# Last steps of a two-layer mixture kernel in another order: the first layer of tiles 30 and 31 half a step ahead, the last convolution and the last h1 product moved forward

## What is computed

```
x  = x + y0 + sum_e alpha_e * (z_e @ B0_e)       # u = x @ [A0 | W0], then mixed over channels per batch
c1 = conv(x) + beta1                             # windows of 12 neighbours, 4 output phases
h1 = c1 @ [A1 | gate]                            # 224 low-rank columns and 28 logits
x  = x + c1 @ W1 + (gate * h1) @ B1
```

## Time and profile before

| what | value |
|---|---|
| median of 3 runs | 404.41 us (402.56 to 407.03) |
| profiled execution, its own time | 404.12 us |
| its span, first to last instruction | 402.3 us |
| mean granted TensorE clock | 0.981 of full |
| PE busy | 382.8 us (95%) |
| DVE busy | 288.2 us (72%) |
| ACT busy | 125.1 us (31%) |

### The profile page before, as it was taken

The page is one execution under the profiler, slowest core; times in us unless marked ns, Lnnn a source line. Parts: engine busy times, 40 slices in busy tenths (PEclk is TensorE's granted clock), DMA queues, the critical chain, the costliest instruction groups (busy, mean ns, idle before and its releaser), DMA issues.

```text
span 402.3 us, 9559 instructions
## 1 busy us (share of the span) xinstructions
PE 382.8 (95%) x3187; PEld 335.7 (83%) x3187; DVE 288.2 (72%) x979; ACT 125.1 (31%) x384; POOL 19.8 (5%) x95
## 2 busy tenths in 40 slices
PE   5977799999999999999999999999999999999976
PEld 4877787888889888888888898888888889877755
DVE  5547688777778777777777887777777778677854
ACT  5335533332233332233222333222332233222310
POOL 5200000000000000000000000000000000000000
PEclk9998879999999999999999999999999999999999
DMA  7756426476777776666677677666666776766651
GB/s 229 230 163 154 94 70 132 122 175 156 181 171 169 183 178 134 164 160 164 150 175 183 156 183 181 155 149 160 160 159 165 179 170 144 159 157 150 142 106 52
DMA packets 70716, 62.97 MB, mean 157 GB/s; under 512 B 3823, under 2 KB 53199, under 8 KB 70570
## 3 DMA queue, kind: packets, MB, share of 16 engines
q1 hardware_dynamic: 70696, 62.74, 64.1%
q10 hardware_dynamic: 2, 0.00, 0.0%
HBM read 45.69 MB, written 16.91 MB: 156 GB/s over the span
## 4 chain that ended last, share of the span: by engine, by line
PE 84%; DVE 7%; DMA 5%; ACT 2%; issue 1%; SPq 1%; DVEq 0%; ACTq 0%
PE p_chy L853 13%; PE p_chy L847 13%; PE p_chy L848 13%; PE p_u L847 9%; PE p_u L853 8%; PE p_u L848 8%; PE p_chy L983 8%; PE p_t L996 3%; DMA win<-x_scratch 3%; PE p_y L847 2%; PE p_y L848 2%; PE p_y L853 2%; DVE mix L623 1%; DMA w_sb<-in_w 1%; DMA x_scratch<-x 1%
## 5 line engine op out<-in xcount | busy, mean ns | idle before, releaser
L847 PE MATMUL p_u<-w_hi,xt_hi 128*128 128x256 f32 (+1 forms) x256 | 72.0, 307 | 2.5 <-DVE w_lo L609 2.5
L848 PE MATMUL p_u<-w_lo,xt_hi 128*128 128x256 f32 (+1 forms) x256 | 69.6, 297 | 0.0
L717 DVE STREAM_TRANSPOSE c<-p_chy 128x512 f32<-128x512 f32 x32 | 22.9, 717 | 56.6 <-PE p_chy L983 56.2
L480 ACT CAST u_hi<-p_u 128x256 fp32r<-128x256 f32 x64 | 24.8, 387 | 107.1 <-PE p_u L853 107.1
L847 PEld LDWEIGHTS p_u<-w_hi,xt_hi 128*128 128x128 f32 x256 | 50.6, 198 | 3.5 <-DVE w_lo L609 1.8
L525 ACT CAST g1t_hi<-p_t 113x256 fp32r<-113x256 f32 x32 | 11.9, 373 | 125.4 <-PE p_t L996 125.4
L848 PEld LDWEIGHTS p_u<-w_lo,xt_hi 128*128 128x128 f32 x256 | 50.7, 198 | 0.0
L847 PE MATMUL p_chy<-w_hi,c_hi 128*128 128x512 f32 x124 | 49.3, 397 | 0.0
L848 PE MATMUL p_chy<-w_lo,c_hi 128*128 128x512 f32 x124 | 48.8, 394 | 0.0
L853 PE MATMUL p_u<-w_hi,xt_lo 128*128 128x256 f32 (+1 forms) x256 | 44.3, 297 | 1.4 <-DVE xt_lo L590 1.4
L983 PEld LDWEIGHTS p_chy<-win,wc_sb 96*32 96x32 f32 x1024 | 26.7, 111 | 17.4 <-issue 12.8
(11 more groups left out here) (165 smaller groups left out, 747.5 us busy)
## 6 DMA issues: line engine op xcount, KB each, us to landing
win<-x_scratch SPq DMA_DIRECT2D x96, 256.0 KB, 4.4
x_scratch<-x SPq DMA_DIRECT2D x32, 260.0 KB, 2.1
xt_sb<-in_xt SPq DMA_DIRECT2D x32, 256.0 KB, 5.3
x_sb<-in_x SPq DMA_DIRECT2D x32, 256.0 KB, 5.3
out<-y_sb SPq DMA_DIRECT2D x32, 256.0 KB, 4.5
w_sb<-in_w SPq DMA_DIRECT2D x4, 256.0 KB, 5.3
w_sb<-in_w SPq DMA_DIRECT2D x1, 1024.0 KB, 7.4
a_sb<-in_a SPq DMA_DIRECT2D x1, 504.0 KB, 3.9
```

The source lines that it names most:

```text
L480: nc.scalar.copy(u_hi[:, t.mod(4), cols], p_u[:, banks]).then_inc(u_hi_done[half], 1)
L717: V.transpose(c1[:], p_cv).then_inc(c1_tr, 1)
L847: mm(psum, lhs_hi, rhs_hi, start=start and n == 0, stop=False)
L848: mm(psum, lhs_hi, rhs_lo, start=False, stop=False)
```

## The change

It touches steps 29 to 34 only; the instructions are the same, in another order. In PE's queue:

- `mixing(30)` moves from the head of step 30 to the end of step 29, between `conv(28)` and `transpose_g1(27)`; `mixing(31)` moves from the head of step 31 into step 30, between the hi and the lo passes of `base_1(28)`.
- In steps 30 and 31 `transpose_g0(s)` now comes right behind `low_rank_1(s-3)`, then `lows_1(s-2)`, then `low_rank_0(s)`, and `base_1(s-2)` only behind that.
- In step 32 `conv(31)` comes right behind `low_rank_1(29)`, ahead of `lows_1(30)` and `base_1(30)`; `lows_1(31)` moves from step 33 into step 32, ahead of `transpose_g1(30)`.
- In step 33 `low_rank_1(30)` lies between the hi and lo passes of `base_1(31)`, and `transpose_g1(31)` behind both.

In DVE's queue `residual(30)` and `residual(31)` move ahead of the chain from L795 to L820 of their step; the layer-0 part of tile 31 (L726 to L750) moves from the head of step 31 to the end of step 30; the transpose and remainder of `c1` of tile 31 move from step 33 to step 32, ahead of the chain of tile 30; `g1t_lo` of tile 30 moves into the chain of tile 31. In ACT's queue the exponent of tile 31 (L533) moves to the end of step 30, and `c1_hi` of tile 31 to step 32. SP's and POOL's queues are as before. In the diff, the part left out on DVE only wraps the instructions of L714 to L750 into functions `c1_transposed`, `c1_low`, `g1t_low`, `z0_logits` and `g0_scaled`.

```diff
--- before.py
+++ after.py
@@ -523,15 +523,24 @@
                 if (s + -3).live():
                     after(act, g1_tr, s, -3)
                     nc.scalar.copy(g1t_hi[:], p_g1t).then_inc(g1t_hi_done, 1)
-                if (s + -LAG).live():
-                    v = s + -LAG
+                def c1_high(v):
+
                     after(act, c1_tr, v)
                     after(act, y1_mm, v, -2)
                     nc.scalar.copy(by_group(c1_hi[:, v.mod(2)]), by_phases(c1)).then_inc(c1_hi_done, 1)
-                if s.live():
-                    after(act, z0_nmax_done, s)
+
+                def z0_exponent(v):
+
+                    after(act, z0_nmax_done, v)
                     nc.scalar.activation(z0_exp[:], by_slot(z0[:])[:, :, R], ACT.Exp, bias=z0_nmax[:],
                                          accum_out=z0_sum[:]).then_inc(z0_exp_done, 1)
+
+                if (s + -LAG).live() and not is_last(s + -LAG):
+                    c1_high(s + -LAG)
+                if is_last(s + -1):
+                    c1_high(s + -1)
+                if s.live() and not is_last(s):
+                    z0_exponent(s)
                 early = at(s, 0) or at(s, 1)
                 if not early and (s + 2).live():
                     mix_high(s + 2)
@@ -549,6 +558,8 @@
                     after(act, ntop_done, s, -LAG)
                     nc.scalar.activation(t_exp[:], top[:, 0:2], ACT.Exp, bias=ntop[:],
                                          accum_out=t_sum[:]).then_inc(t_exp_done, 1)
+                if at(s, NT - 2):
+                    z0_exponent(s + 1)
                 if t.live():
                     u_high(t, "a")
                 if at(s, 0):
...
+
+                ahead = at(s, NT - 2) or is_last(s)
+                if (s + -LAG).live() and not is_last(s + -LAG):
+                    c1_transposed(s + -LAG)
+                if (s + -3).live() and not is_last(s + -LAG):
+                    g1t_low(s + -3)
+                if s.live() and not is_last(s):
+                    z0_logits(s)
+                    if at(s, 0):
+                        mix_low(s + 1)
+                if (s + -LAG).live() and not is_last(s + -LAG):
+                    c1_low(s + -LAG)
+                if s.live() and not is_last(s):
+                    g0_scaled(s)
                 if at(s, 0):
 
                     u_low(s + 1, "b")
@@ -776,6 +803,11 @@
                     u_low(s + 3, "a")
                 if (s + -3).live() and not is_last(s + -LAG):
                     output(s + -3)
+                if ahead:
+                    residual(s)
+                if is_last(s + -1):
+                    c1_transposed(s + -1)
+                    c1_low(s + -1)
                 early = at(s, 0) or at(s, 1)
                 if not early and (s + 4).live():
                     xt_low(s + 4)
@@ -803,6 +835,8 @@
                     V.max_index(top_i[:], top[:], h1[:, L1N:H1N]).then_inc(top_i_done, 1)
                     after(dve, top_i_done, v)
                     V.tensor_copy(top_f[:], top_i[:, 0:2]).then_inc(top_f_done, 1)
+                    if is_last(v):
+                        g1t_low(s + -3)
                     after(dve, t_exp_done, v)
                     V.reciprocal(t_rec[:], t_sum[:]).then_inc(t_rec_done, 1)
                     after(dve, t_rec_done, v)
@@ -823,10 +857,13 @@
                                     ALU.mult).then_inc(g1_done, 1)
                 if is_last(s + -LAG):
                     output(s + -3)
+                if at(s, NT - 2):
+                    z0_logits(s + 1)
+                    g0_scaled(s + 1)
                 if not early and (s + UA).live():
                     u_low(s + UA, "b")
                     u_low(s + UA, "a")
-                if not early and s.live():
+                if not early and not ahead and s.live():
                     residual(s)
                 if at(s, 2):
                     dve.wait_ge(b1_hi_done, 1)
@@ -1028,23 +1065,47 @@
                     between()
                     lo_passes(y1_bank(v), full, False)
 
-                if s.live():
+                if at(s, NT - 3):
                     mixing(s)
-                if is_last(s + -LAG):
-
+                    low_rank_1(s + -3)
                     lows_1(s + -LAG)
+                    transpose_g0(s)
+                    base_1(s + -LAG, lambda: low_rank_0(s))
+                    conv(s + -1)
+                    mixing(s + 1)
+                    transpose_g1(s + -LAG)
+                elif at(s, NT - 2) or is_last(s):
                     low_rank_1(s + -3)
-                    base_1(s + -LAG, lambda: transpose_g1(s + -LAG))
+                    transpose_g0(s)
+                    lows_1(s + -LAG)
+                    low_rank_0(s)
+                    if is_last(s):
+                        base_1(s + -LAG)
+                    else:
+                        base_1(s + -LAG, lambda: mixing(s + 1))
+                    conv(s + -1)
+                    transpose_g1(s + -LAG)
+                elif is_last(s + -1):
+                    low_rank_1(s + -3)
+                    conv(s + -1)
+                    lows_1(s + -LAG)
+                    base_1(s + -LAG)
+                    lows_1(s + -1)
+                    transpose_g1(s + -LAG)
+                elif is_last(s + -LAG):
+                    base_1(s + -LAG, lambda: low_rank_1(s + -3))
+                    transpose_g1(s + -LAG)
                     low_rank_1(s + -LAG)
                 else:
-                    if (s + -3).live() and not is_last(s + -3):
+                    if s.live():
+                        mixing(s)
+                    if (s + -3).live():
                         low_rank_1(s + -3)
                     if (s + -LAG).live():
                         lows_1(s + -LAG)
                     early = at(s, 0) or at(s, 1)
                     t = s + (s.c + 1 if early else UA)
-                    running = t.live()
-                    if running:
+                    if t.live():
                         u_half(t, "b")
                         transpose_g0(s)
                         u_half(t, "a")
@@ -1056,20 +1117,13 @@
                                 pe.wait_ge(rsw0_done, 1)
                                 column_sums(p_rs1, P, a1_hi, a1_lo).then_inc(rs1_mm, 1)
                             u_half(t + 1, "a")
-                    elif s.live():
-                        transpose_g0(s)
                     if at(s, 2):
                         pe.wait_ge(w1_lo_done, 1)
                         after(pe, c1_tr, s, -2)
                         column_sums(p_rsw1, 1, w1_hi, w1_lo).then_inc(rsw1_mm, 1)
                     if (s + -LAG).live():
-                        if not running and s.live():
-                            base_1(s + -LAG, lambda: low_rank_0(s))
-                        elif is_last(s + -1):
-                            base_1(s + -LAG, lambda: conv(s + -1))
-                        else:
-                            base_1(s + -LAG)
-                    if (s + -1).live() and not is_last(s + -1):
+                        base_1(s + -LAG)
+                    if (s + -1).live():
                         conv(s + -1)
                     if (s + -LAG).live():
                         transpose_g1(s + -LAG)
```

More of the change, by code:

```diff
@@ L709, in residual, with c1_transposed @@
                                     x_sb[:, v.mod(4), :].rearrange("p (f q) -> p f q", f=NPH), ALU.add).then_inc(x1_done, 1)
-                if (s + -LAG).live():
-                    v = s + -LAG
+                def c1_transposed(v):
                     after(dve, cv_mm, v)
@@ L717, in step, with c1_low @@
                     V.transpose(c1[:], p_cv).then_inc(c1_tr, 1)
-                if (s + -3).live():
-                    after(dve, g1t_hi_done, s, -3)
-                    V.tensor_tensor(g1t_lo[:], p_g1t, g1t_hi[:].bitcast(f32), ALU.subtract).then_inc(g1t_lo_done, 1)
-                if s.live():
[L723 to L733, removed]
+                def c1_low(v):
                     after(dve, c1_hi_done, v)
@@ L736, in step, with g1t_low, z0_logits @@
                                     by_group(c1_hi[:, v.mod(2)].bitcast(f32)), ALU.subtract).then_inc(c1_lo_done, 1)
-                if s.live():
-                    after(dve, z0_exp_done, s)
+                def g1t_low(v):
+                    after(dve, g1t_hi_done, v)
+                    V.tensor_tensor(g1t_lo[:], p_g1t, g1t_hi[:].bitcast(f32), ALU.subtract).then_inc(g1t_lo_done, 1)
+                def z0_logits(v):
+                    after(dve, z0_mm, v)
+                    if at(v, 0):
+                        dve.wait_ge(z_add_done, 1)
+                    V.tensor_tensor(z0[:], p_z0, z_add[:, v.n(), :], ALU.add).then_inc(z0_done, 1)
+                    after(dve, z0_done, v)
+                    V.tensor_reduce(z0_nmax[:], by_slot(z0[:])[:, :, R], X, ALU.max, negate=True).then_inc(z0_nmax_done, 1)
@@ L739, in step, with g0_scaled @@
+                def g0_scaled(v):
```

(11 more changed lines are left out.)

1 line of the change is left out of this document (removed).

## The result

| | before | after |
|---|---|---|
| median of 20 runs each | 404.46 us | 408.27 us |
| ratio after / before | | 1.0095, 95% interval 1.0069 to 1.012 |
| profiled execution / its span | 404.12 / 402.3 us | 412.1 / 410.2 us |
| `conv(28)` to the last y_sb, in the profile | 37.15 us | 42.06 us |

A forecast was written before the change was run, and what follows sets the result against it. PE, busy 95% of the span, was taken as the bound through how its in-order queue is filled. The forecast was 404.12 + 2.2 (order) + 1.6 (clock) = 407.9 us, range 404.3 to 409.9.

The forecast's parts named there:

- End of step 29 and step 30: low_rank_1(27) starts 0.94 us after transpose_g1(27); PE then idles 0.86 us ahead of transpose_g0(30), waiting for DVE's g0s.
- Step 31: g1t_lo(28) queues behind tile 31's z0 work on DVE; low_rank_0(31) starts near 378.05, 0.4 us later than before.
- Tile 31's hand-over: residual(31) ends 0.4 us earlier, at 379.2; 8.35 us of store, issues and landing lead to conv(31) at 387.55.
- the rival of earlier windows: Windows land earlier than 8.35 us after x1, near 386, hiding the extra work; time 404.8 us, chance 0.09.
- Step 32: PE idles 2.6 us ahead of conv(31); from there 13.75 us to y_sb, against 11.16 before.
- The order term: Last y_sb comes 2.2 us later, at 401.3, from the new block order and its waits.
- The clock term: The 2.6 us idle at conv(31) drops the clock to half rate for 3.4 us, costing 1.6 us.
- the long one: Low clock for 6.8 us from the wait at conv(31), costing 3.4 us; time 409.7 us, chance 0.08.
- The sum: The profiled execution's 404.12 us plus 2.2 for order and 1.6 for the clock, giving 407.9 us.
- The clock staying up: The wait at conv(31) is shorter or brings no clock drop; time 406.3 us, chance 0.27.
- The half step is really won: The 3.0 us of new waits vanish and low_rank_0(31) starts at 375.05; time 403.3 us, chance 0.06.
- its break-even: low_rank_0(31) starting at 375.9, with fixed lengths of 23.2 us from there to y_sb.

The follow-up runs named there:

- The run with the covers put back: The half step alone, with transpose_g1(27) before mixing(30), lows_1(28) before transpose_g0(30), low_rank_0(30) amid the hi passes; 404.01 us against 404.22, ratio 1.000.
- the kernels with 0.40 and 1.33 us of idle: The change with ten unused matmuls ahead of conv(31), ratio 1.0053; the change with lows_1(30) ahead of conv(31), ratio 1.0055.
- the filled kernel: The change with ten unused 512-wide matmuls between low_rank_1(29) and conv(31); 405.73 us, ratio to before 1.0053; again 406.22 us, ratio 1.0043.
- the three edits: Kernel before with residual(s) amid the gate chain, low_rank_0(s) amid the hi passes, tile 31's c1_hi and c1_lo earlier; 400.67 us, again 400.52.
- the half step alone: The change with PE steps 32 and 33, and tile 31's c1 work on ScalarE and VectorE, as before; 403.23 us against 403.33, ratio 1.0024.

## Why the prediction held, and where a size was off

- **End of step 29 and step 30: right.** `low_rank_1(27)` started 0.84 after `transpose_g1(27)` (0.94 foreseen) and waited 0.46; the idle ahead of `transpose_g0(30)` was 0.72, foreseen as 0.86, and released by DVE's `g0s`.
- **Step 31: right in mechanism, a little too dark.** `g1t_lo(28)` stood behind tile 31's `z0` work; `low_rank_0(31)` came 0.2 later than before, not 0.4. The run with the covers put back shows that these waits, and no transfer, held it.
- **Tile 31's hand-over: right.** From the end of the residual, 381.92, to `conv(31)` at 390.34 it took 8.42; I had 8.35. `conv(31)` came 0.55 earlier than before against 0.4 foreseen. The output store was issued at 380.35 and x1's at 381.94, and its price was indeed near nothing. This also answers the rival of earlier windows: they landed no sooner after x1 than before.
- **Step 32: right.** Idle 2.71 against 2.6. From `conv(31)` to the last y_sb at full clock 13.67, against 13.75.
- **The order term** is then 39.06 - 37.15 = 1.9 us; I had 2.2. The 0.3 is the 0.2 of step 31 and the 0.1 behind `conv(31)`.
- **The clock term: right in mechanism, with a price that depends on the execution.** It was priced at 1.6, from a stretch of 3.4 us, and the long one got a chance of 0.08. The second trace of the change shows the short one, at 1.54; the trace of after shows the long one, at 2.95. One in two traces does not give the odds, but it speaks against 0.08. Two things led there. The prediction took the wait at 46.90 for 2.4 us, from its stretch; on PE it is 2.74, so the new wait was not "on the long side of both" but at the longer one, which had 6.8 us behind it. And it took dense matmuls behind the wait as the reason for a short stretch. The first thing behind it is `conv`, in both traces of the change, so the kind of work does not tell the two lengths apart:

```profile
49.59 1.94 PE L983 MATMUL p_chy<-win,wc_sb 96*32 96x128 f32 x32 [2.74 <-DVE rs L774]
```

- **What does tell them apart in the traces** is when the clock falls. Each of the 14 traces has a wait of 1.95 us or more ahead of a `conv` near 50 us (shown above: that of before), and three have one at `conv(31)`. Read in half-microsecond stretches, the clock fell while PE still stood in 10 of these 17 waits (2.71 to 2.76 us, and 5.10), and stayed low for 6.8 us in each. In the other 7 (1.95 to 2.65 us) it fell as `conv` began or later, and stayed low for 3.4. The two waits of the change, 2.71 and 2.65, are one of each kind. Why a few hundredths of a microsecond in the wait decide this is not shown.
- **The sum.** The forecast's 2.2 + 1.6 and the measured 3.8 agree better than the parts do, and that is luck: the order term was 0.3 too high, and the clock's price was 1.54 in one trace and 2.95 in the other. The medians leave 3.8 - 1.9 = 1.9 for the clock, 0.9 to 2.9 by the interval, too wide to say which price is the usual one. How often each length occurs stays open, as only two executions of the change have a trace.
- **The rivals.** The clock staying up needed a shorter wait, or a filled one; the kernels with 0.40 and 1.33 us of idle show it, at ratios of 1.0053 and 1.0055. "The half step is really won" is refuted for the change as it stands. The fixed lengths of its break-even hold: in the filled kernel the end comes 398.54 - 375.36 = 23.18 after `low_rank_0(31)`, foreseen as 23.2. No run brought `low_rank_0(31)` far enough forward in the change's own order to test the break-even itself.

## What to carry to other kernels

A block may be moved ahead only so far as the data it waits for is there: moving a consumer of a late transfer ahead of ready work does not bring the transfer forward, it takes the cover away. When a block is moved on one queue, list what it was hiding on the others; here `mixing` hid ScalarE's copy and `lows_1` hid VectorE's chain, and three waits of 0.5 to 0.7 us, with a late `g1t_lo`, ate the 1.9 us of matmuls that `low_rank_0(31)` no longer had to wait for. At the end of a pipelined kernel, find the last hand-over (here residual to store to windows, over 8 us of fixed length) and bring forward what it starts from. A wait on PE can cost a second time, by the clock: those of 2.65, 2.71 and 5.10 us at `conv(31)` did, while one of 2.40 us near the start of the three edits' first trace did not:

```profile
27.86 0.31 PE L973 MATMUL p_t<-ident_r,g0s 128*101 128x128 f32 x1 [2.40 <-DVE g0s L760]
```

```profile
27.90:31.00 3.10, 3.10 (x25) 3.10 (x26) 0.89 (x3) 1.37 (x4) 0.19 (x1) 1.00 0.02 5
```

## What the runs showed of the hardware that was not expected

- Ten matmuls whose results nobody reads keep the clock up and shorten the tail: 13.67 beside 15.21 and 16.62 us from `conv(31)` to the last y_sb. The medians are 406.22 beside 407.99 us on one chip.
- The same kernel shows low stretches of 3.4 and 6.8 us behind nearly the same wait (2.65 and 2.71 us), at prices of 1.54 and 2.95. Of 17 waits ahead of a `conv`, the stretch was 6.8 us in the 10 where the clock fell before `conv` began, and 3.4 us in the 7 where it fell later.
- In the traces with PE idles of 0.29 to 1.85 us at `conv(31)` the clock stayed at 1.00 there; with 2.65, 2.71 and 5.10 it fell to 0.50.
- The granted clock in the first 28 us of a trace can read 1.00 while the matmuls run at half pace: eight 512-wide ones took 0.63 us each at a reading of 1.00 in the trace of after, and 0.63 at a reading of 0.50 in that of the half step alone:

```profile
22.80:26.40 3.60, 3.60 (x9) 2.82 (x10) 1.18 (x7) 0.00 (x0) 0.19 (x1) 1.00 0.79 176
22.80:26.40 3.60, 3.60 (x9) 2.85 (x10) 1.18 (x7) 0.00 (x0) 0.19 (x1) 0.50 0.74 183
```
